# Query and gate products of a decoder's memory layer as three 16-bit products instead of one fp32 product

## The chip, the cores and the metric

The kernel runs on one core of one Trainium2 chip. The metric is the device time of one execution in microseconds (us); lower is better. Three runs of the kernel before are shown, and one execution taken with the hardware profiler.

## The reference

Two decoder layers over x of 8 batch rows x 256 tokens x 256 features, each sublayer with a layer norm of its input and a residual. In order: self-attention with 16 heads of 128; linear cross-attention over a context of 64 tokens; a feed-forward layer whose weights are rounded to 16 levels; attention over features; the memory layer; a feed-forward layer with ternary weights. The memory layer is what the change touches:

```
x = rmsnorm(hidden_states, norm_w)              # var over features, eps 1e-6, times norm_w
q = (x @ wq.T).reshape(B, L, NH, HD)            # 16 heads of 16
k = (memory_tokens @ wk.T).reshape(B, M, NH, HD)
v = (memory_tokens @ wv.T).reshape(B, M, NH, HD)
attn = jnp.einsum('blhd,bmhd->bhlm', q, k) * scale
attn = softmax(jnp.where(memory_mask[:, None, None, :], attn, -inf))
out = jnp.einsum('bhlm,bmhd->blhd', attn, v).reshape(B, L, C) @ wo.T
gate = jax.nn.sigmoid(x @ wg.T)
return gate * out
```

Here hidden_states is the layer norm of the running x, and wq and wg are 256x256.

## The kernel before

The program has two parts with a barrier between them.

**attention_part** does the self-attention: 16 heads times 4 pairs of batch rows are 64 steps (and two more, since the work of a step is spread over three). Steps 0 to 10 and 59 to 65 are written out, 11 to 58 are a loop of six rounds of eight. In step i, TensorE makes query and key products of step i, scores of step i-1 (L1124) and the value product of step i-2 (lines 75 to 77, through `pair_matmuls`), then column sums (L1153, L1155). VectorE takes the row maximum of the scores (L906), ScalarE the exponentials (L596), GpSimd splits them into exp_hi (L483) and exp_lo (L485), and VectorE adds four tiles into X (L931). TensorE's scores of the next step wait for the exponentials, whose banks they use. Much is tucked into the steps: preparing the next head's weights; the 16-level rounding (`level_part`, on VectorE, only in the loop); and, in numbered steps, scales and halves of the later layers' matrices. Such a block stands on VectorE at the end of its step, behind the four X updates. At step 60 that is L970, the lower halves of the key-value products of the linear layer. In the last steps VectorE also takes statistics of the first batch rows (L843) and normalises them (L855: tiles ctx_t, k_t). A maximum over all partitions goes through DRAM: SyncE writes the partitions' maxima out and reads them back to every partition.

A matrix "split" is scaled so that its largest value is 64, rounded to fp16 (the upper half), and the rest rounded to fp16 (the lower half). A product of two split operands is three fp16 matmuls into the same bank:

```
nc.tensor.matmul(out, lhs[0], rhs[0], start=first, stop=False)
nc.tensor.matmul(out, lhs[0], rhs[1], start=False, stop=False)
return nc.tensor.matmul(out, lhs[1], rhs[0], start=False, stop=last)
```

**streams_part** does the other five layers for each batch row alone: `lin`, `ffn`, `fat`, `mem`, `ter`. Four rows are under way at once (a group: rows 0 to 3, then 4 to 7), each with its own buffers and two of the eight banks, PA and PB. The order of the work on each engine is not written by hand. The list `work` gives the stages of one row, each with its engine, a length in us and what it comes after; `turns_by_engine` puts them in order for all rows by earliest start, and between equals by urgency, in which `LEAD * (STREAMS - b % STREAMS)` favours the earlier rows of a group.

In the memory layer a row goes so: stats, aggr, eps (VectorE), pow (GpSimd), xn (VectorE), turn (TensorE, L1688: four transposes), xt (ScalarE, L1401: two copies out of the bank, scaled by norm_w, into fp32), mem_q and mem_g (TensorE, L1673 and L1680: four fp32 matmuls of 256 columns each), qt and ge (ScalarE, L1445 and L1448). Then, for each of two tiles of 128 tokens: s (L1797, L1802: scores), max, sub, exp, sum, rd (L1623, L1626, L1452, L1630, L1633), pn (GpSimd, L1379), pt (L1810: transposes), pte, o, ote; and at the end mem_out, mem_go and mem_add. The layers `ffn` and `ter` already have a split input: ScalarE's copy to fp16 (L1405) and VectorE's lower half, `xt_stream<-banks,xt_stream` (L1527).

## Time and profile before

| | us |
|---|---|
| median of three runs | 922.98 (921.57 to 923.1) |
| the profiled execution, its own time | 921.72 |
| its span, first to last instruction | 919.9 |
| TensorE (PE) busy, matmuls | 854.1 (93%) |
| VectorE (DVE) busy | 729.0 (79%) |
| ScalarE (ACT) busy | 520.4 (57%) |
| GpSimd (POOL) busy | 369.3 (40%) |
| share of the chain that ended last: PE, DVE | 23%, 12% |

The share of busy time is an average over both parts. "Idle before" is the time in which an engine had nothing to run just ahead of an instruction, with the engine and tile that ended it. A merged row such as "1.73 PE banks L1673 x8" gives how long the chain stayed on that line: the profiler records each fp32 matmul as two, so x8 is four matmuls. Matmul rows overlap: a single one is listed with 0.27 us though the next starts 0.11 later, so lengths of products are read from the chain.

### The profile page before, as it was taken

Reading aid. Unit: us, or ns where it says so; the run is one execution under the profiler, and the core shown is the slowest. Engines: PE = TensorE matmul, PEld = TensorE weight load, DVE = VectorE, ACT = ScalarE, POOL = GpSimd, SP = SyncE. Lnnn points to the kernel's source line nnn. Section 1 sums busy time; section 2 is a strip of 40 time slices with the busy share of each in tenths; the row PEclk is TensorE's granted clock in tenths of the full one; section 3 lists DMA queues with packets and bytes.
Section 4 is the critical chain, followed back from the end, with each engine's and each line's share of the span. In section 5 each row is a group of like instructions: output and inputs, shape, how many; then the busy total and the mean of one; then the engine's idle time right before and its main releaser. Section 6 shows DMA issues by size and latency. Waiting matters only on the chain. (4 is left out here: it accounts for less than half of the span.)

```text
span 919.9 us, 18693 instructions
## 1 busy us (share of the span) xinstructions
PE 854.1 (93%) x6868; PEld 633.9 (69%) x6868; DVE 729.0 (79%) x1775; ACT 520.4 (57%) x1245; POOL 369.3 (40%) x354
## 2 busy tenths in 40 slices
PE   4788988999999999999999998999988889999786
PEld 3455766777777777777777776887855578787554
DVE  6748868878888788778887775897799779887895
ACT  1435576656665666556655745464464964535556
POOL 4103456545554455455555554053233032521410
PEclk9799999999999999999999999999999999999999
DMA  9122331011101110011000000000000010000001
GB/s 279 38 71 69 54 95 35 2 35 35 34 0 34 34 34 8 27 34 34 14 21 11 1 1 1 1 2 1 1 2 1 8 40 1 1 1 1 1 1 46
DMA packets 34722, 25.56 MB, mean 28 GB/s; under 512 B 9492, under 2 KB 31596, under 8 KB 34668
## 3 DMA queue, kind: packets, MB, share of 16 engines
q1 hardware_dynamic: 34380, 24.56, 10.2%
q8 instruction: 35, 0.57, 0.3%
q10 hardware_dynamic: 288, 0.26, 0.1%
q14 instruction: 19, 0.16, 0.1%
HBM read 22.65 MB, written 2.17 MB: 27 GB/s over the span
## 5 line engine op out<-in xcount | busy, mean ns | idle before, releaser
L483 POOL CAST exp_hi<-exp_scores 128x1024 f16<-128x1024 f32 x64 | 67.1, 1048 | 212.5 <-ACT exp_scores L596 212.5
L485 POOL TENSOR_TENSOR exp_lo<-exp_scores,exp_hi 128x1024 f16<-128x1024 f32 x64 | 140.7, 2198 | 5.1
L596 ACT ACTIVATE exp_scores<-banks,exp_bias,unscale 128x256 f32<-128x256 f32 x256 | 141.2, 560 | 2.1
L75 PE MATMUL banks<-value_out_hi,xn_t_hi 128*128 128x256 f16 x512 | 139.6, 273 | 0.2 <-DVE X L931 0.2
L77 PE MATMUL banks<-value_out_hi,xn_t_lo 128*128 128x256 f16 x512 | 139.6, 273 | 0.0
L76 PE MATMUL banks<-value_out_lo,xn_t_hi 128*128 128x256 f16 x512 | 139.6, 273 | 0.0
L1124 PE MATMUL banks<-qk 128*128 128x256 f32 x512 | 121.6, 380 | 9.0 <-ACT exp_scores L596 8.9
L1124 PEld LDWEIGHTS banks<-qk 128*128 128x128 f32 x512 | 96.6, 190 | 30.3 <-issue 9.6
L931 DVE SCALAR_TENSOR_TENSOR X<-banks,colsum,X 128x256 f32<-128x256 f32 x256 | 106.2, 477 | 11.0 <-DVE colsum L922 9.6
L575 ACT ACTIVATE qk<-banks 128x512 f32<-128x512 f32 x128 | 75.8, 601 | 57.6 <-PE banks L77 57.6
L906 DVE TENSOR_REDUCE neg_rowmax<-banks 128x4 f32<-128x1024 f32 x64 | 78.2, 1221 | 27.9 <-PE banks L1124 27.9
L75 PE MATMUL banks<-xn_t_hi,head_weights_hi 128*128 128x512 f16 x256 | 96.9, 378 | 0.6 <-issue 0.6
L77 PE MATMUL banks<-xn_t_hi,head_weights_lo 128*128 128x512 f16 x256 | 97.0, 379 | 0.0
L76 PE MATMUL banks<-xn_t_lo,head_weights_hi 128*128 128x512 f16 x256 | 96.9, 379 | 0.0
L1368 POOL TENSOR_TENSOR rstd_stream<-rstd_stream,neg_half 128x2 f32<-128x2 f32 x36 | 26.5, 737 | 138.1 <-DVE rstd_stream L1517 127.1
L592 ACT ACTIVATE exp_bias<-neg_rowmax,unscale 128x4 f32<-128x4 f32 x64 | 18.8, 293 | 100.3 <-DVE neg_rowmax L906 100.3
L76 PEld LDWEIGHTS banks<-value_out_lo,xn_t_hi 128*128 128x128 f16 x512 | 50.1, 98 | 11.8
L75 PEld LDWEIGHTS banks<-value_out_hi,xn_t_hi 128*128 128x128 f16 x512 | 50.1, 98 | 9.1 <-DVE X L931 2.5
L1379 POOL TENSOR_TENSOR big_stream<-big_stream,den_stream 128x1024 f32<-128x1024 f32 x16 | 30.4, 1903 | 60.0 <-DVE den_stream L1633 60.0
L77 PEld LDWEIGHTS banks<-value_out_hi,xn_t_lo 128*128 128x128 f16 x512 | 50.1, 98 | 5.8
L442 POOL TENSOR_TENSOR head_weights_lo<-head_weights,head_weights_hi 128x512 f16<-128x512 f32 x32 | 38.9, 1218 | 31.5 <-ACT head_weights_hi L507 31.4
L596 ACT ACTIVATION_READ_ACCUMULATOR exp_scores<-banks,exp_bias,unscale 128x1 f32 x256 | 50.7, 198 | 0.0
(251 smaller groups left out, 1964.7 us busy)
## 6 DMA issues: line engine op xcount, KB each, us to landing
head_weights<-in_wqkv_d SPq DMA_DIRECT2D x32, 128.0 KB, 3.8
weight_absmax_rows<-across_partitions SPq DMA_DIRECT2D x15, 256.0 KB, 4.3
X<-in_x_d SPq DMA_DIRECT2D x4, 512.0 KB, 7.7
head_weights<-in_wqkvt_d SPq DMA_DIRECT2D x16, 128.0 KB, 3.6
head_weights<-in_w_o_d SPq DMA_DIRECT2D x16, 128.0 KB, 3.6
out<-X SPq DMA_DIRECT2D x8, 256.0 KB, 2.1
ternary_then_kv_and_rows<-in_c_fc_d SPq DMA_DIRECT2D x1, 1024.0 KB, 5.1
ternary_then_kv_and_rows<-in_c_proj_d SPq DMA_DIRECT2D x1, 1024.0 KB, 7.9
```

The lines of the kernel that those rows point to most:

```text
L75: nc.tensor.matmul(out, lhs[0], rhs[0], start=first, stop=False)
L76: nc.tensor.matmul(out, lhs[0], rhs[1], start=False, stop=False)
L77: return nc.tensor.matmul(out, lhs[1], rhs[0], start=False, stop=last)
L442: nc.gpsimd.tensor_tensor(wlo[:, u, 2 * a:2 * a + 2], wst[:, u, 2 * a:2 * a + 2], whi[:, u, 2 * a:2 * a + 2], ALU.subtract).then_inc(wlo_r ...
L483: nc.gpsimd.tensor_copy(probh[:, s1_.par], prob[:, s1_.par]).then_inc(exph_ready, 1)
L485: nc.gpsimd.tensor_tensor(probl[:, s1_.par], prob[:, s1_.par], probh[:, s1_.par], ALU.subtract).then_inc(expl_ready, 1)
L575: nc.scalar.activation(qk[:, st.par, s, :], qk_ps[s], ACT.Copy).then_inc(qk_ready, 1)
L596: last = nc.scalar.activation(prob[:, s1_.par, t, :], sc_ps[t // ST][:, t % ST, :], ACT.Exp, bias=nbias[:, t:t + 1], scale=unscale[:, s1_. ...
L906: nc.vector.tensor_reduce(nmax[:, :], sc_both, AX.X, ALU.max, negate=True).then_inc(nmax_ready, 1)
L931: last = nc.vector.scalar_tensor_tensor(out=g.X[:, TP * s2.p + t, :], in0=xm_ps[t // ST][:, t % ST, :], scalar=csum[:, t:t + 1], in1=g.X[: ...
L1124: last = nc.tensor.matmul(sc_ps[b][:, t, :], qk[:, s1_.par, 0, q], qk[:, s1_.par, 1, kk], start=True, stop=True)
L1379: nc.gpsimd.tensor_tensor(by_head(s), by_head(s), den[s][:, t, :].unsqueeze(2).broadcast_to([P, XH, M]), ALU.mult).then_inc(mem_pn[t], 1)
```

## The change

Seven things:
- `mem_q` and `mem_g` multiply split x with split wq1 and wg1: 12 fp16 matmuls each for four fp32 ones.
- norm_w goes into the two matrices (they are multiplied by it in place), so x is copied unscaled, as in `ffn` and `ter`: ScalarE's upper half, and a new VectorE stage `mem_lo` for the lower half.
- At the end of steps 59, 61 and 62 of the head loop (`KV_HI` is 59) VectorE scales the matrices by norm_w and takes their maxima; makes scales; and makes the lower halves. ScalarE makes the upper halves in step 62. SyncE carries the maxima through DRAM.
- The scale is taken out again in the copies `mem_qt` and `mem_ge`.
- Two tables of partition maxima (`ternary_rows`, `nf4_max_rows`) now share memory with two buffers of `level_part`, which are used at other times; the new table lies there too.
- The planner's list has the new stages and lengths.
- `LEAD` goes from 2.0 to 2.5.

```
@@ -48,7 +48,7 @@
-HOP, LEAD = 0.15, 2.0
+HOP, LEAD = 0.15, 2.5
@@ -190,7 +188,14 @@
-    part = [sb("nf4_part0", [P, CHUNK * BLK], BF16), sb("nf4_part1", [P, CHUNK * BLK], BF16)]
+    part = [sb("nf4_part0_or_rows", [P, CHUNK * BLK], BF16), sb("nf4_part1_or_rows", [P, CHUNK * BLK], BF16)]
+    trows, mrows = (t[:, 0:P * 2 * 2].bitcast(F32).rearrange("p (q s) -> p q s", s=2) for t in part)
+    mem_rows = trows
+    mem_max = sb("mem_w_max", [P, 2])
+    mem_all = sb("mem_w_max_all", [P, 2])
+    mem_scale = sb("mem_w_scale", [P, 2])
+    mem_weights = [w[:, :, :].rearrange("p k n -> p (k n)") for w in (g.wq1, g.wg1)]
+    mem_parts = [[t[:, :, :].rearrange("p k n -> p (k n)") for t in pair] for pair in g.mem_halves]
@@ -434,6 +441,10 @@
+        sp.wait_ge(mem_max_ready, 2)
+        sp.dma_start(spread(6, P, 2), mem_max[:, :]).then_inc(mem_max_out, 16)
+        sp.wait_ge(mem_max_out, 16)
+        sp.dma_start(mem_rows.rearrange("p q s -> p (q s)"), gathered(6, P, 2)).then_inc(mem_max_in, 16)
@@ -605,6 +616,10 @@
+            if known(i) and i == KV_HI + 3:
+                act.wait_ge(mem_step, 5)
+                for n, (w, (hi, _)) in enumerate(zip(mem_weights, mem_parts)):
+                    nc.scalar.activation(hi, w, ACT.Copy, scale=mem_scale[:, n:n + 1]).then_inc(mem_hi_ready, 1)
@@ -964,6 +979,35 @@
+            if i == KV_HI:
+                dve.wait_ge(late_loads, 16 * len(g.small_loads))
+                for w in (g.wq1, g.wg1):
+                    for k in range(KT):
+                        nc.vector.tensor_scalar(w[:, k, :], w[:, k, :], g.normw[:, k:k + 1], None,
+                                                ALU.mult).then_inc(mem_normed, 1)
+                for n, w in enumerate(mem_weights):
+                    dve.wait_ge(mem_normed, KT * (n + 1))
+                    nc.vector.tensor_reduce(mem_max[:, n:n + 1], w, AX.X, ALU.max,
+                                            apply_absolute_value=True).then_inc(mem_max_ready, 1)
+            if i == KV_HI + 2:
+                dve.wait_ge(mem_max_in, 16)
+                nc.vector.tensor_reduce(mem_all[:, :], mem_rows.rearrange("p q s -> p s q"), AX.X,
+                                        ALU.max).then_inc(mem_step, 1)
+                dve.wait_ge(mem_step, 1)
+                nc.vector.tensor_scalar(mem_all[:, :], mem_all[:, :], 1e-30, None, ALU.max).then_inc(mem_step, 1)
+                dve.wait_ge(mem_step, 2)
+                nc.vector.reciprocal(mem_scale[:, :], mem_all[:, :]).then_inc(mem_step, 1)
+                nc.vector.tensor_scalar(g.mem_unscale[:, :], mem_all[:, :], 1.0 / SPLIT_TOP, None, ALU.mult)
+                nc.vector.tensor_scalar(g.mem_half_unscale[:, :], mem_all[:, 1:2], 0.5 / SPLIT_TOP, None,
+                                        ALU.mult).then_inc(mem_step, 1)
+                dve.wait_ge(mem_step, 3)
+                nc.vector.tensor_scalar(mem_scale[:, :], mem_scale[:, :], SPLIT_TOP, None, ALU.mult).then_inc(mem_step, 1)
+            if i == KV_HI + 3:
+                dve.wait_ge(mem_hi_ready, 2)
+                for n, (w, (hi, lo)) in enumerate(zip(mem_weights, mem_parts)):
+                    nc.vector.scalar_tensor_tensor(out=lo, in0=w, scalar=mem_scale[:, n:n + 1], in1=hi, op0=ALU.mult,
+                                                   op1=ALU.subtract)
@@ -1321,8 +1364,8 @@
-    work += norm_work("mem", "fat_add", ["xt ACT .74"])
-    work += ["mem_q PE 1.8", "mem_kbd DVE .67 fat_add", "mem_g PE 1.74 mem_xt", "mem_qt ACT .49 mem_q", "mem_ge ACT .49 mem_g"]
+    work += norm_work("mem", "fat_add", ["xt ACT .49", "lo DVE .6"])
+    work += ["mem_q PE 1.36", "mem_kbd DVE .67 fat_add", "mem_g PE 1.36 mem_lo", "mem_qt ACT .49 mem_q", "mem_ge ACT .49 mem_g"]
@@ -1396,13 +1439,8 @@
-                elif layer == "mem":
-                    for k in range(KT):
-                        last = nc.scalar.activation(xt[s][:, k, :], tiles(PA[s])[:, k, :], ACT.Copy,
-                                                    scale=g.normw[:, k:k + 1])
-                    last.then_inc(mem["xt_ready"], 1)
-                    nc.scalar.activation(xh[s], tiles(PA[s]), ACT.Copy).then_inc(ffn_hi if layer == "ffn" else ter_hi, 1)
+                    nc.scalar.activation(xh[s], tiles(PA[s]), ACT.Copy).then_inc(xt_hi[layer], 1)
@@ -1442,10 +1480,10 @@
-                nc.scalar.activation(qt[s][:, :, :], tiles(PB[s]), ACT.Copy).then_inc(mem_q, 1)
+                nc.scalar.activation(qt[s][:, :, :], tiles(PB[s]), ACT.Copy, scale=g.mem_unscale[:, 0:1]).then_inc(mem_q, 1)
-                nc.scalar.activation(gate[s][:, :, :], tiles(PA[s]), ACT.Tanh, scale=0.5).then_inc(mem_g, 1)
+                nc.scalar.activation(gate[s][:, :, :], tiles(PA[s]), ACT.Tanh, scale=g.mem_half_unscale[:, :]).then_inc(mem_g, 1)
@@ -1522,8 +1560,8 @@
-            elif part == "lo" and layer in ("ffn", "ter"):
-                dve.wait_ge(ffn_hi if layer == "ffn" else ter_hi, n[s])
+            elif part == "lo":
+                dve.wait_ge(xt_hi[layer], n[s])
@@ -1774,9 +1812,19 @@
-                features_first(PB[s], g.wq1, xt[s]).then_inc(mem_q_full, 1)
+                for m in range(KT):
+                    for k in range(KT):
+                        last = pair_matmuls(nc, tiles(PB[s])[:, m, :],
+                                            [w[:, k, m * P:(m + 1) * P] for w in g.mem_halves[0]],
+                                            [x[:, k, :] for x in (xh[s], xl[s])], k == 0, k == KT - 1)
+                last.then_inc(mem_q_full, 1)
-                tokens_first(PA[s], xt[s], g.wg1).then_inc(mem_g_full, 1)
+                for t in range(ST):
+                    for k in range(KT):
+                        last = pair_matmuls(nc, tiles(PA[s])[:, t, :],
+                                            [x[:, k, t * P:(t + 1) * P] for x in (xh[s], xl[s])],
+                                            [w[:, k, :] for w in g.mem_halves[1]], k == 0, k == KT - 1)
+                last.then_inc(mem_g_full, 1)
@@ -1980,6 +2028,9 @@
+    g.mem_halves = [[sb(f"mem_w{n}_{half}", [P, KT, D], F16) for half in ("hi", "lo")] for n in range(2)]
+    g.mem_unscale = sb("mem_w_unscale", [P, 2])
+    g.mem_half_unscale = sb("mem_w_half_unscale", [P, 1])
```

Where the new blocks stand on VectorE, in the steps 61 and 62: before, from the X updates of step 61 to the statistics of step 63 (L931 is an X update, L906 a row maximum).

```order
L931 SCALAR_TENSOR_TENSOR X<-banks,colsum,X 128x256 x4
L889 RECIPROCAL rowsum_inverse<-rowsum 128x4
L891 RECIPROCAL rowsum_inverse_halves<-rowsum 128x4
L906 TENSOR_REDUCE neg_rowmax<-banks 128x4
L919 TENSOR_SCALAR colsum_raw<-banks,unscale 128x4
L922 SCALAR_TENSOR_TENSOR colsum<-banks,unscale,colsum_raw 128x4
L931 SCALAR_TENSOR_TENSOR X<-banks,colsum,X 128x256 x4
L889 RECIPROCAL rowsum_inverse<-rowsum 128x4
L891 RECIPROCAL rowsum_inverse_halves<-rowsum 128x4
L843 BN_STATS ln_stats<-X 128x6 x4
```

And now; a maximum and a clamp of the first block stand ahead of these rows.

```order
L1000 RECIPROCAL mem_w_scale<-mem_w_max_all 128x2
L1001 TENSOR_SCALAR mem_w_unscale<-mem_w_max_all 128x2
L1002 TENSOR_SCALAR mem_w_half_unscale<-mem_w_max_all 128x1
L1005 TENSOR_SCALAR mem_w_scale<-mem_w_scale 128x2
L904 RECIPROCAL rowsum_inverse<-rowsum 128x4
L906 RECIPROCAL rowsum_inverse_halves<-rowsum 128x4
L921 TENSOR_REDUCE neg_rowmax<-banks 128x4
L934 TENSOR_SCALAR colsum_raw<-banks,unscale 128x4
L937 SCALAR_TENSOR_TENSOR colsum<-banks,unscale,colsum_raw 128x4
L946 SCALAR_TENSOR_TENSOR X<-banks,colsum,X 128x256 x4
L1009 SCALAR_TENSOR_TENSOR mem_w_lo<-wq,mem_w_scale,mem_w_hi 128x512
L1009 SCALAR_TENSOR_TENSOR mem_w_lo<-wg,mem_w_scale,mem_w_hi 128x512
```

What moved: nothing; six instructions came in behind the X updates of step 61, and two behind those of step 62, ahead of the reciprocals and of the row maximum of step 63.

On TensorE, in the memory layer of the first group, before: scores of row 1, transposes of row 3's input, scores of row 2, query and gate product of row 3, and only then row 0: its probabilities turned (L1810), scores of row 3, row 0's output (L1817).

```order
L1797 MATMUL banks<-mask_bias,ones 128x512 x2
L1802 MATMUL banks<-big_stream,qt_stream 128x256 x4
L1688 MATMUL banks<-ident,xn_stream 128x128 x4
L1797 MATMUL banks<-mask_bias,ones 128x512 x2
L1802 MATMUL banks<-big_stream,qt_stream 128x256 x4
L1673 MATMUL banks<-xt_stream,wq 128x256 x4
L1680 MATMUL banks<-wg,xt_stream 128x256 x4
L1810 MATMUL banks<-ident,big_stream 128x128 x8
L1797 MATMUL banks<-mask_bias,ones 128x512 x2
L1802 MATMUL banks<-big_stream,qt_stream 128x256 x4
L1817 MATMUL banks<-mid_stream,v 32x128 x8
```

And now, from behind row 1's scores and row 2's gate product on:

```order
L1858 MATMUL banks<-ident,big_stream 128x128 x8
L1845 MATMUL banks<-mask_bias,ones 128x512 x2
L1850 MATMUL banks<-big_stream,qt_stream 128x256 x4
L1726 MATMUL banks<-ident,xn_stream 128x128 x4
L1865 MATMUL banks<-mid_stream,v 32x128 x8
L1845 MATMUL banks<-mask_bias,ones 128x512 x2
L1850 MATMUL banks<-big_stream,qt_stream 128x256 x4
L75 MATMUL banks<-xt_stream,mem_w_hi 128x256
L76 MATMUL banks<-xt_stream,mem_w_hi 128x256
```

Row 0's probabilities (L1858) come ahead of row 2's scores, and row 0's output (L1865) and the scores of its second tile (the second L1850) ahead of row 3's query product, of which the first two matmuls are shown. The second group has the same order.

## Rows read from the trace of the kernel before

**Rows 1.** Stretches: length; busy us (instructions) of PE, PEld, DVE, ACT, POOL; clock, DMA, GB/s
```profile
50.00:540.00 490.00, 477.94 (x3855) 350.29 (x3854) 390.07 (x928) 296.13 (x814) 244.98 (x213) 1.00 0.13 31
645.00:665.00 20.00, 19.75 (x107) 16.65 (x107) 14.09 (x41) 9.10 (x20) 4.65 (x5) 1.00 0.00 1
665.00:715.00 50.00, 41.93 (x362) 28.96 (x358) 45.08 (x81) 27.69 (x37) 16.49 (x11) 1.00 0.01 1
...
840.00:890.00 50.00, 41.93 (x353) 29.60 (x353) 43.91 (x80) 26.04 (x35) 16.50 (x11) 0.97 0.00 1
```

**Rows 2.** The chain that ended last: start, us, engine and line, instructions
```profile
777.97 1.75 PE banks L1742 x16
...
836.72 1.73 PE banks L1673 x8
838.45 1.73 PE banks L1680 x8
```

**Rows 3.** Timeline of ScalarE, second group's memory layer: start us, us
```profile
821.07 0.83 ACT L1401 ACTIVATE xt_stream<-banks,normw 128x256 f32<-128x256 f32 x2
```

**Rows 4.** Groups by line, 580 to 920: busy us, mean ns; idle before
```profile
L1527 DVE TENSOR_TENSOR xt_stream<-banks,xt_stream 128x512 f16<-128x512 f32 x16 | 10.9, 680 | 0.0
...
L1405 ACT ACTIVATE xt_stream<-banks 128x512 f16<-128x512 f32 x16 | 9.5, 596 | 19.3 <-PE banks L1688 18.7
```

**Rows 5.** Timeline of the memory layer, first group: start us, us
```profile
661.27 1.90 POOL L1379 TENSOR_TENSOR big_stream<-big_stream,den_stream 128x1024 f32<-128x1024 f32 x1 [9.10 <-DVE den_stream L1633]
...
671.14 1.04 PE L1810 MATMUL banks<-ident,big_stream 128*128 128x128 f32 x8
```

**Rows 6.** Timeline of VectorE, last steps of the head loop
```profile
517.18 1.66 DVE L931 SCALAR_TENSOR_TENSOR X<-banks,colsum,X 128x256 f32<-128x256 f32 x4
...
520.95 1.22 DVE L906 TENSOR_REDUCE neg_rowmax<-banks 128x4 f32<-128x1024 f32 x1 [1.96 <-PE banks L1124]
...
537.44 1.23 DVE L906 TENSOR_REDUCE neg_rowmax<-banks 128x4 f32<-128x1024 f32 x1 [1.87 <-PE banks L1124]
...
541.01 1.66 DVE L931 SCALAR_TENSOR_TENSOR X<-banks,colsum,X 128x256 f32<-128x256 f32 x4
...
544.78 1.23 DVE L906 TENSOR_REDUCE neg_rowmax<-banks 128x4 f32<-128x1024 f32 x1
545.92 1.37 DVE L855 TENSOR_SCALAR ctx_t<-X,ln_mean_var,ln_rstd 128x256 f32<-128x256 f32 x4
...
556.16 3.22 DVE L855 TENSOR_SCALAR k_t<-X,ln_mean_var,ln_rstd 128x256 f32<-128x256 f32 x4
```

**Rows 7.** Timeline of GpSimd, the same steps
```profile
518.66 2.13 POOL L485 TENSOR_TENSOR exp_lo<-exp_scores,exp_hi 128x1024 f16<-128x1024 f32 x1
...
526.12 4.30 POOL L485 TENSOR_TENSOR exp_lo<-exp_scores,exp_hi 128x1024 f16<-128x1024 f32 x1
...
542.62 2.13 POOL L485 TENSOR_TENSOR exp_lo<-exp_scores,exp_hi 128x1024 f16<-128x1024 f32 x1
...
556.13 2.13 POOL L485 TENSOR_TENSOR exp_lo<-exp_scores,exp_hi 128x1024 f16<-128x1024 f32 x1
```

**Rows 8.** VectorE's groups by line and shape, whole span
```profile
L664 DVE TENSOR_SCALAR weight_absmax_all<-weight_absmax_all 128x4 f32<-128x4 f32 x16 | 13.0, 814 | 0.6
...
L970 DVE SCALAR_TENSOR_TENSOR ternary_then_kv_and_rows<-kv,lin_scale,ternary_then_kv_and_rows 128x128 f16<-128x128 f32 x1 | 2.6, 2630 | 0.0
...
L958 DVE TENSOR_REDUCE lin_max<-wq 128x1 f32<-128x512 f32 x1 | 0.7, 677 | 0.0
```

**Rows 9.** Timeline of TensorE's scores of steps 61 and 63, and of ScalarE's last exponential before
```profile
535.44 1.97 PE L1124 MATMUL banks<-qk 128*128 128x256 f32 x8 [0.93 <-ACT exp_scores L596]
...
548.46 0.20 ACT L596 ACTIVATION_READ_ACCUMULATOR exp_scores<-banks,exp_bias,unscale 128x1 f32 x1
...
548.81 1.97 PE L1124 MATMUL banks<-qk 128*128 128x256 f32 x8
```

**Rows 10.** DMA issues: number, size, median us to landing
```profile
weight_absmax_rows<-across_partitions SPq DMA_DIRECT2D x15, 256.0 KB, 4.3
```

9 lines of the change are left out of this document (4 added, 5 removed).

## The prediction

> **What bounds the kernel now.** I read the stretches first, to see which engine is full where. In the head loop it is TensorE: 477.94 of the 490 us from 50 to 540 [rows 1]. In the second part eight batch rows go through five layers, four at a time, and each group has two kinds of stretch. Where its memory layer begins (645 to 665), TensorE is busy 19.75 of 20 us and VectorE 14.09. Then VectorE leads: 45.08 of 50 us from 665 to 715, with TensorE at 41.93; the second group repeats this (43.91 and 41.93 from 840 to 890) [rows 1]. The chain that ended last says the same: in the first kind of stretch it is made of the products themselves, 1.73 us for the query product and 1.73 for the gate product [rows 2]. So a shorter product is worth its whole length in one stretch and nothing by itself in the other, where VectorE's length and the order decide.
>
> **The products.** Each of the 16 (a query and a gate for each batch row) is now four fp32 matmuls in 1.73 us. Sixteen matmuls of 16 bits, 256 columns wide, took 1.75 us in the feed-forward layer, 0.109 each [rows 2]. Twelve of them are 1.31 us: 0.42 saved per product, 3.4 per group, 6.7 in all.
>
> **The new lower half of x.** ScalarE's two scaled copies (0.83 us) [rows 3] become one of 0.60, as the feed-forward layer has it, and VectorE gets a subtraction of 0.68, whose input from the banks is like that of the ternary layer's [rows 4]. ScalarE wins 0.23 for each batch row, VectorE pays 0.68: 2.7 us per group. Between a row's transposes and its query product the chain grows by about 0.5 us (0.68 less 0.23, and a hand-over). TensorE has other rows' products there, so I count nothing for the wait. In the stretch where TensorE is full, VectorE had 5.9 idle us [rows 1]; two of the four subtractions fit there, the other two fall where VectorE leads: +1.4 per group.
>
> **The order.** The planner gets new lengths, and LEAD goes from 2.0 to 2.5, which favours the earlier row of a group. The second excerpt of the order shows the effect: row 0's probabilities are transposed, and its second tile's scores made, ahead of row 3's query product. In the trace those probabilities were ready when the GpSimd multiplication that starts at 661.27 and takes 1.90 us was done, but TensorE turned them only at 671.14 [rows 5]: 8 us of waiting in the queue. That work now goes in about 7 us earlier and can fill VectorE's idle time, which is 5.9 and 4.9 us in the two stretches [rows 1]. How much of these 10.8 us it fills no row shows. The bounds are 0, less if the new order stalls where the old one did not (a rival below), and about 5, half of it. I take 2.3, nearer the low end, since two more VectorE instructions now stand in front of the same softmax.
>
> Per group: six of the eight products lie in the full stretch, -2.5; the last row's two I count at nothing; +1.4; -2.3. That is -3.4, and -6.8 for both groups. Scaling the copies of query and gate by a column instead of a constant is free: both are one instruction as before.
>
> **The end of the head loop.** The splitting of the two matrices is not free. VectorE gets three blocks, each behind the four X updates of a step, and the first excerpt of the order shows two of them. GpSimd computes exp_lo at those very moments, and the trace shows what this does. Four scalings of 128x256 took 1.37 us at 545.92, but 3.22 at 556.16, when exp_lo ran from 556.13 [rows 6, 7]. The 128x128 subtraction of the key-value halves took 2.63 us, and the exp_lo beside it 4.30 where it takes 2.13 elsewhere [rows 7, 8]. So an instruction waits until the other engine's is over.
> - Step 59, from 518.8: exp_lo runs from 518.66 to 520.79 [rows 7], so the four scalings start at 520.8 and take 1.1 more; two maxima at 0.68 [rows 8] end at 523.3. The next row maximum, at 520.95 after an idle 1.96 [rows 6], comes 2.6 us later. Most of it is absorbed; some 0.8 reaches step 61, where TensorE already waited 0.93 us for the exponentials [rows 9]. Bounds 0 and 1.5; I take 0.8.
> - Step 61, from 534.7: a maximum over 256 values, well under the 0.68 of one over 512, a clamp of 0.81 like L664, and four small ones: 1.8 us. The row maximum there had been idle 1.87, after 0.56 for the exponentials [rows 6, 8]. Counted at nothing. Its input crosses SBUF through DRAM in two transfers; even two of the 4.3 us that the big one takes [rows 10] end by 532, before it is wanted. SyncE queues nothing behind them but the end.
> - Step 62, from 542.6: two lower halves of 128x512, some 0.65 each by the 0.68 of a same-sized one [rows 4], against an exp_lo that starts at 542.62 [rows 7]. Whoever is first, the second of the two ends only after exp_lo: about 546.0, 3.4 us late. Here is no slack: the row maximum at 544.78 had no idle time before it [rows 6], and the scores of the last step start at 548.81, as the exponentials end [rows 9]. Bounds: 1.4 (no contention) and 4.0. I take 3.4. ScalarE's two upper halves, 1.2 us, run while it has nothing else due.
>
> What the Trainium skill says speaks against this change: its page "SBUF — State Buffer", section "Who interferes with whom", has the port pair that VectorE and GpSimd share as an exclusive lock, taken also by a VectorE instruction with two SBUF inputs, and issue order decides who blocks. By that rule step 62 costs its 3.4, and the maxima of steps 59 and 61 are not held up; the trace agrees with the first half in the 2.63 us above, and no row here tests the second by itself.
>
> **The sum.** -6.8 + 0.8 + 3.4 = -2.6 us. The profiled execution took 921.72 (a span of 919.9 and 1.8 around it), which gives 919.1; the median of three runs is 922.98, 1.26 above the profiled one, so the forecast is **920.4 us**.
>
> **Rivals.**
> - *The order pays more* (0.22). The whole of half the idle time is filled and the lower halves of x fit in: per group -2.5 - 3.8, with the head's end -8.4: 914.6. For it: 8 us of waiting work [rows 5]. Against it: the stretch from 665 is a chain of softmax stages over few banks, not loose work.
> - *VectorE takes over* (0.30). All four subtractions per group (2.7 us) delay VectorE's softmax, TensorE's saving turns into waiting for it, and only row 0's two products (0.84), which stand before the first scores, come off. Per group +1.9, with the head's end +7.9: 930.9; the order filling part of it gives some 927. It decides from the point where VectorE's idle time between 645 and 665 is under 3 us. For it: VectorE is at 90% from 665 on [rows 1]. This is the case on the other side.
> - *The port costs less than I think* (0.06): the two lower halves slip in before exp_lo, 1.4 for 4.2 at the head's end: 917.6. Against it: the rows above.
> - *Three 16-bit matmuls are not cheaper* (0.02): with a weight load that does not overlap (0.1 each), 12 would take 2.5 us instead of 1.73, +12 us. The 16 in 1.75 us, each with its own load, speak against it.
>
> **How the numbers follow.** The forecast has 0.40; the bounds of its terms give it 917 to 924. About 0.2% is what a measurement of this kernel can tell from no change, 1.85 us here. Within the forecast's case 0.22 is faster by more than that, 0.14 within it, 0.04 slower; the order that pays and the cheap port are faster (0.28); of VectorE's case 0.05 is within and 0.25 slower; the last is slower. Together 0.50, 0.19 and 0.31. The range reaches from the order's case, 914, to most of VectorE's, 929.
>
> **What would show it.** In the new profile: query and gate products of 1.31 us in the chain; a row maximum of step 63 that starts some 5.6 us after the X updates of step 62 where it was 2.2; the head's end at about 567 instead of 563; VectorE's idle time in the memory stretch down, and each group about 3.4 us shorter. It is wrong if the head's end moves by less than 2 us, or if a group becomes longer, with TensorE waiting for VectorE's softmax.

## The result and the profile after

The changed kernel takes **923.01 us** (921.02 to 926.96, 22 runs), the kernel before 922.13 (920.07 to 923.41, 22 runs) beside it: a ratio of 1.0019, interval 1.0010 to 1.0028. It is slower by 0.9 us; the forecast was 2.6 faster. The profiled execution took 921.02, its span is 919.2; it is the fastest of the 22, so its trace shows the changed kernel at its best.

The page's busy times, where before PE had 854.1 and DVE 729.0:

```profile
PE 847.3 (92%) x6932; PEld 628.3 (68%) x6932; DVE 743.2 (81%) x1797; ACT 519.1 (56%) x1239; POOL 367.9 (40%) x354
```

TensorE has 6.8 us less to do, near 16 times 0.42, and the kernel is not faster. I divide the time at the first VectorE instruction of the second part, a product on `headmask`. For the part ahead of it I count from the row maximum of step 59: that takes out the prologue, which moves by up to 2.8 us between the traced executions (the row maximum of step 59 starts between 512.12 and 514.92). These are the two ends of that stretch, before and after.

```profile
513.49 1.23 DVE L906 TENSOR_REDUCE neg_rowmax<-banks 128x4 f32<-128x1024 f32 x1
...
564.82 1.27 DVE L1489 TENSOR_TENSOR headmask<-headmask 128x4 f32<-128x4 f32 x1 [1.65 <-PEq L1926]
```

```profile
512.25 1.23 DVE L921 TENSOR_REDUCE neg_rowmax<-banks 128x4 f32<-128x1024 f32 x1
...
568.81 1.27 DVE L1527 TENSOR_TENSOR headmask<-headmask 128x4 f32<-128x4 f32 x1 [1.69 <-PEq L1974]
```

The stretch, called the **head's end** from here on, went from 51.33 to 56.56 us: +5.2. The **second part**, from `headmask` to the start of the last update of X, went from 352.06 (564.82 to 916.88) to 347.38 (568.81 to 916.19): -4.7.

VectorE at the head's end, after; its columns are start, length, engine, line, operands, and the idle time before in brackets:

```profile
517.51 2.46 DVE L987 TENSOR_SCALAR wq<-wq,normw 128x256 f32<-128x256 f32 x2
519.89 0.60 DVE L987 TENSOR_SCALAR wg<-wg,normw 128x256 f32<-128x256 f32 x2
520.42 0.67 DVE L991 TENSOR_REDUCE mem_w_max<-wq 128x1 f32<-128x512 f32 x1
...
521.75 1.19 DVE L921 TENSOR_REDUCE neg_rowmax<-banks 128x4 f32<-128x1024 f32 x1
...
525.00 3.81 DVE L1014 SCALAR_TENSOR_TENSOR ternary_then_kv_and_rows<-kv,lin_scale,ternary_then_kv_and_rows 128x2048 f16<-128x2048 f32 x2
...
529.25 1.21 DVE L921 TENSOR_REDUCE neg_rowmax<-banks 128x4 f32<-128x1024 f32 x1
...
534.38 0.17 DVE L1000 RECIPROCAL mem_w_scale<-mem_w_max_all 128x2 f32<-128x2 f32 x1
534.46 2.09 DVE L1001 TENSOR_SCALAR mem_w_unscale<-mem_w_max_all 128x2 f32<-128x2 f32 x1
...
536.75 1.19 DVE L921 TENSOR_REDUCE neg_rowmax<-banks 128x4 f32<-128x1024 f32 x1
...
541.85 2.71 DVE L1009 SCALAR_TENSOR_TENSOR mem_w_lo<-wq,mem_w_scale,mem_w_hi 128x512 f16<-128x512 f32 x1 [0.99 <-ACT mem_w_hi L622]
544.48 0.74 DVE L1009 SCALAR_TENSOR_TENSOR mem_w_lo<-wg,mem_w_scale,mem_w_hi 128x512 f16<-128x512 f32 x1
...
547.19 1.22 DVE L921 TENSOR_REDUCE neg_rowmax<-banks 128x4 f32<-128x1024 f32 x1
...
554.72 1.23 DVE L921 TENSOR_REDUCE neg_rowmax<-banks 128x4 f32<-128x1024 f32 x1 [2.65 <-PE banks L1168]
```

GpSimd beside it:

```profile
517.41 2.14 POOL L496 TENSOR_TENSOR exp_lo<-exp_scores,exp_hi 128x1024 f16<-128x1024 f32 x1
...
534.40 2.13 POOL L496 TENSOR_TENSOR exp_lo<-exp_scores,exp_hi 128x1024 f16<-128x1024 f32 x1
541.88 2.13 POOL L496 TENSOR_TENSOR exp_lo<-exp_scores,exp_hi 128x1024 f16<-128x1024 f32 x1
```

Measured from the row maximum of step 59, the next ones came 2.0 us later than before (step 60), then 0.9 earlier (61), 0.5 later (62), 3.7 later (63) and 5.2 later (64). For before, [rows 6] has those of steps 60, 62 and 63, that of step 64 starts at 550.81, and that of step 61 is this one:

```profile
531.43 1.20 DVE L906 TENSOR_REDUCE neg_rowmax<-banks 128x4 f32<-128x1024 f32 x1
```

Three VectorE instructions end with an exp_lo or just behind it: the first pair of scalings (2.46 us, the second pair 0.60), a scaling of 128x2 at 534.46 (2.09 us, where the reciprocal before it took 0.17) and the first lower half (2.71 us, the second 0.74). The last row maximum waits 2.65 us for TensorE. Here is why, in TensorE's scores of step 62 and 63 and in stretches of 5 us (length; busy us of PE, PEld, DVE, ACT, POOL; clock):

```profile
541.03 1.89 PE L1168 MATMUL banks<-qk 128*128 128x256 f32 x8
...
551.21 3.48 PE L1168 MATMUL banks<-qk 128*128 128x256 f32 x8 [3.98 <-ACT exp_scores L607]
```

```profile
545.00:550.00 5.00, 2.05 (x33) 1.39 (x31) 4.90 (x19) 1.53 (x6) 1.21 (x2) 1.00 0.01 3
550.00:555.00 5.00, 3.79 (x11) 2.86 (x12) 2.26 (x8) 2.36 (x6) 3.32 (x3) 0.66 0.00 0
```

TensorE was busy 2.05 of 5 us and idle 3.98 before the scores; then its granted clock was 0.66 over 550 to 555, so half speed (1.2 GHz) for most of it, and the scores took 3.48 instead of 1.89 us. Before, all four stretches from 540 to 560 had clock 1.00.

The second part. The products have the length that was forecast: the query product of row 0 starts at 653.50, the gate product at 654.81, the next transposes at 656.12, 1.31 us each.

```profile
653.50 0.27 PE L75 MATMUL banks<-xt_stream,mem_w_hi 128*128 128x256 f16 x1
...
654.81 0.27 PE L75 MATMUL banks<-mem_w_hi,xt_stream 128*128 128x256 f16 x1
...
656.12 1.24 PE L1726 MATMUL banks<-ident,xn_stream 128*128 128x128 f32 x8
```

The stretches where before VectorE had 5.9 and 4.9 idle us [rows 1] (counted from `headmask` they lie 4.0 us earlier here), and VectorE's group of lower halves, whose last number is the idle time before them:

```profile
645.00:665.00 20.00, 19.75 (x142) 16.21 (x142) 17.90 (x49) 8.41 (x18) 2.09 (x3) 1.00 0.00 1
665.00:715.00 50.00, 40.80 (x378) 28.93 (x374) 46.36 (x82) 26.68 (x35) 19.01 (x13) 1.00 0.00 1
```

```profile
L1565 DVE TENSOR_TENSOR xt_stream<-banks,xt_stream 128x512 f16<-128x512 f32 x24 | 16.2, 677 | 0.7 <-ACT xt_stream L1443 0.7
```

VectorE is busy 17.90 of 20 us where it was 14.09, with 24 instead of 16 of these subtractions in the whole part, and waited only 0.7 us for their input.

### The profile page after: what moved, and what is told of

Same layout as the page of the kernel before. It is cut to its first block and busy times, and to the rows that moved or that the text cites. A ratio compares the mean times of both kernels' runs of the same rounds, so it can differ in the third digit from the quotient of the medians.

```text
span 919.2 us, 18839 instructions
## 1 busy us (share of the span) xinstructions
PE 847.3 (92%) x6932; PEld 628.3 (68%) x6932; DVE 743.2 (81%) x1797; ACT 519.1 (56%) x1239; POOL 367.9 (40%) x354
## 5 line engine op out<-in xcount | busy, mean ns | idle before, releaser
L496 POOL TENSOR_TENSOR exp_lo<-exp_scores,exp_hi 128x1024 f16<-128x1024 f32 x64 | 138.6, 2165 | 5.1
```

The costliest lines, as they stand in the source:

```text
L496: nc.gpsimd.tensor_tensor(probl[:, s1_.par], prob[:, s1_.par], probh[:, s1_.par], ALU.subtract).then_inc(expl_ready, 1)
```

## The experiments

The medians stand beside the same kernel before, measured with them: 922.13 for the change, 921.55 to 921.75 in the four batches of the others. The ratios take that out. Below, "head's end" and "second part" are read from each run's trace as above: one execution for each kernel, where a median has several.

| kernel | median, us | ratio, interval | head's end | second part |
|---|---|---|---|---|
| before | 921.6 | | 51.33 | 352.06 |
| the change | 923.01 | 1.0019 (1.0010 to 1.0028) | 56.56 | 347.38 |
| no split | 917.68 | 0.9952 (0.9935 to 0.9968) | 51.36 | 347.77 |
| split alone | 928.63 | 1.0076 (1.0062 to 1.0091) | 56.84 | 353.58 |
| change, LEAD 2.0 | 929.22 | 1.0077 (1.0062 to 1.0091) | 56.83 | 354.16 |
| before, LEAD 2.5 | 932.70 | 1.0122 (1.0107 to 1.0138) | 51.32 | 359.56 |
| blocks moved | 918.49 | 0.9955 (0.9942 to 0.9968) | 51.41 | 349.07 |
| blocks of 61, 62 moved | 917.72 | 0.9959 (0.9946 to 0.9973) | 50.83 | 348.47 |
| blocks and key-value halves moved | 916.03 | 0.9949 (0.9931 to 0.9966) | 50.24 | 347.29 |
| the same, LEAD 3.0 | 917.00 | 0.9947 (0.9929 to 0.9965) | 50.23 | 349.78 |
| 16 matmuls a product | 928.41 | 1.0069 (1.0056 to 1.0082) | 56.81 | 353.75 |
| short lower half | 922.27 | 1.0007 (0.9995 to 1.0020) | 56.71 | 346.72 |
| old order | 941.92 | 1.0222 (1.0205 to 1.0239) | 56.60 | 367.00 |
| old order, no lower half | 929.18 | 1.0068 (1.0048 to 1.0088) | 56.82 | 353.37 |
| new order alone | 922.16 | 0.9998 (0.9987 to 1.0010) | 51.31 | 352.60 |

The head's end repeats within 0.3 us between kernels that have it alike. The second part does not repeat so well: the split alone has the second part of before, stage for stage, and took 1.5 us longer, in an execution where TensorE's clock was 0.93 from 690 to 715 and from 865 to 890 (before: 1.00 and 0.98). So of the second part a difference under 1.5 us in one trace says little. The clock has a large share in this. I cut each second part into slices of 5 us and counted the time at half speed from the granted clock: 6.9 us before, 6.6 in the change, 6.9 with the new order alone, 6.8 without the split, 10.0 with the split alone, 9.9 with 16 matmuls, 10.0 in the change with LEAD 2.0, 20.5 before with LEAD 2.5, 19.7 in the old order and 13.4 there without the lower half. As an estimate, a microsecond at half speed costs at most half a microsecond (the scores above took 3.48 us for 1.89). Between executions of one kernel it shows too: of the 22 runs of the change those with a mean granted clock of 0.983 took 924.9 to 927.0 us, those with 0.987 or more 921.0 to 923.0.

### Which part costs, which earns

**No split.** The changed kernel without its three blocks, their transfers and ScalarE's upper halves; the matrices' halves hold a constant. It leaves out the scaling and splitting of the two matrices.

```
-            if i == KV_HI:
...
-            if i == KV_HI + 2:
...
-            if i == KV_HI + 3:
...
+        for t in (*mem_parts[0], *mem_parts[1], g.mem_unscale[:, :], g.mem_half_unscale[:, :]):
+            nc.gpsimd.memset(t, 0.5)
```

> The changed kernel without the three blocks and their transfers: the halves are filled with a constant at the start, so the products have the same length and wrong values; nothing else differs. Theory A (the second part earns 4.7 us, the head's end gives it back): 922.1 - 4 to 5.5, so 916.6 to 918.1. Theory B (the second part earns nothing): 922 to 923. If the blocks' cost and this gain do not add up to the change's +0.9 within 1 us, the two parts act on each other.

**Split alone.** The kernel before with the blocks, transfers and upper halves added, and nothing of it used: the second part is the old one, with its copies scaled by norm_w (which so counts twice in the output). Its diff against the kernel before is the change's own, of the parts before `streams_part`.

> The kernel before with the three blocks that scale, split and measure the two matrices at the head loop's end (and their transfers), but with the second part, its planner and its order as before; since the second part still multiplies by norm_w, that weight is applied twice. Theory A (the blocks cost what they look like in the new profile, mostly by waiting for GpSimd's exp_lo): 922.1 + 4 to 5.5, so 926 to 927.6, and in the profile the head loop ends 4 to 5 us later. Theory B (the blocks are hidden and the new profile only looks late by chance, and the second part earns nothing): 922 to 923.2.

The first came out as expected of theory A, the second 1.0 us above its range. The split costs 5.2 to 5.5 us at the head's end, and the change earns 3.9 in the second part by the medians (917.68 against 921.55), 4.3 by the traces. But the two do not add up. By the medians the split costs 7.1 us in the kernel before and 5.3 in the new one (923.01 less 917.68), and 7.1 less 3.9 is 3.2, not 0.9: by the expectation's own measure the two parts act on each other. The trace of the split alone shows where. Its row maxima in the first group keep step with those of before up to the seventh (118.85 and 118.92 us into the second part), and the eighth is 1.5 late. Between them TensorE had the same two waits in both kernels (1.76 and 0.63 us), and then its scores took this long, here and in the kernel before:

```profile
693.17 1.91 PE L1846 MATMUL banks<-big_stream,qt_stream 64*128 64x256 f32 x8
```

```profile
688.40 1.03 PE L1802 MATMUL banks<-big_stream,qt_stream 64*128 64x256 f32 x8
```

The granted clock was 0.67 from 690 to 695 in the one and 1.00 from 686 to 691 in the other; the transposes and the mask ahead of the scores lost 0.7 us as well. Why the clock fell in one execution and not in the other after the same waits, no run shows.

**LEAD back to 2.0** in the changed kernel, and **LEAD 2.5** in the kernel before, each one line:

```
-HOP, LEAD = 0.15, 2.5
+HOP, LEAD = 0.15, 2.0
```

> The changed kernel with LEAD back at 2.0. Theory A (shorter products and the planner's new lengths earn it, LEAD next to nothing): within 0.8 of the changed kernel, 922.2 to 923.8. Theory C (LEAD brings the earlier rows forward and earns at least a third of the second part's 4.7): 924.5 to 926. Theory D (LEAD costs, since the last row of each group ends later): 920 to 922.

> The kernel before with LEAD 2.5 alone. Theory A: within 0.8 of before, 921.3 to 922.9. Theory C: 919 to 920.6. Theory D: 923 to 925.

Both lose, and by more than any of the theories allowed: 6.2 us against the change, 11.1 against before. In the trace of the second, its fastest run by 4.3 us, 7.5 us are lost, and up to 6.8 of them by the estimate above are the clock's (20.5 us at half speed where before had 6.9). LEAD has no direction of its own; with the planner's lengths it picks one of many orders. Each of the two kernels has the order that suits it, and a neighbour costs more than the whole change. VectorE's lower halves show part of it, with LEAD 2.0: 5.3 us of waiting where the change has 0.7.

```profile
L1565 DVE TENSOR_TENSOR xt_stream<-banks,xt_stream 128x512 f16<-128x512 f32 x24 | 16.4, 682 | 5.3 <-ACT xt_stream L1443 5.2
```

### The head's end

**The blocks moved.** Each block stands right behind the row maximum of its own step, ahead of the X updates, instead of behind them and ahead of the row maximum of the next step (and ScalarE's upper halves ahead of the exponentials of the last step):

```
+            if known(i) and i == KV_HI:
...
+            if known(i) and i == KV_HI + 2:
...
+            if known(i) and i == KV_HI + 3:
...
             if runs(i, 2):
                 for t in range(TP):
...
-            if i == KV_HI:
...
-            if i == KV_HI + 2:
...
-            if i == KV_HI + 3:
...
```

> The changed kernel with its three VectorE blocks (steps 59, 61, 62) standing behind the next row maximum instead of ahead of it, where VectorE has idle time and no exp_lo runs on GpSimd; ScalarE's two upper halves go ahead of the exponentials of the last step. Theory A (a block costs by its place: it stands in front of a row maximum that the last scores need, and behind an exp_lo of GpSimd): the same instructions elsewhere cost 0 to 1.5 us over the kernel without them (917.7), so 917.7 to 919.2, and the second part starts 0 to 1.5 us later than the 564.7 of that kernel; the two lower halves take about 1.5 us together, none over 1.0. Rival B (blocks cost their busy length of about 7 us wherever they stand, for instance because VectorE is what the head's end waits for, or because the two upper halves on ScalarE now delay the exponentials): 921 to 923, second part at 567 or later.

What is called the next row maximum there is that of the block's own step: by the code and the trace the blocks went forward. 918.49, and a head's end of 51.41, as without the split (51.36): **the same instructions cost nothing where they stand now.** VectorE in steps 59, 61 and 62 of this kernel:

```profile
514.92 1.23 DVE L921 TENSOR_REDUCE neg_rowmax<-banks 128x4 f32<-128x1024 f32 x1
516.06 1.25 DVE L927 TENSOR_SCALAR wq<-wq,normw 128x256 f32<-128x256 f32 x2
...
534.71 0.15 DVE L941 TENSOR_SCALAR mem_w_unscale<-mem_w_max_all 128x2 f32<-128x2 f32 x1
...
538.87 1.23 DVE L921 TENSOR_REDUCE neg_rowmax<-banks 128x4 f32<-128x1024 f32 x1 [1.59 <-PE banks L1168]
540.01 0.74 DVE L949 SCALAR_TENSOR_TENSOR mem_w_lo<-wq,mem_w_scale,mem_w_hi 128x512 f16<-128x512 f32 x1
540.67 0.75 DVE L949 SCALAR_TENSOR_TENSOR mem_w_lo<-wg,mem_w_scale,mem_w_hi 128x512 f16<-128x512 f32 x1
```

The scalings take 1.25 instead of 2.46 us, the scaling of 128x2 0.15 instead of 2.09, the lower half 0.74 instead of 2.71; and from 545 to 560 TensorE's clock is 1.00 throughout. The next row maximum comes as soon as its scores are there, since a block now stands in time in which VectorE would wait for TensorE's column sums (1.89 us in step 59 and 1.78 in step 62 of the kernel before). The move changed two things at once: the blocks no longer stand directly ahead of a row maximum, and they hardly meet an exp_lo any more (the first scalings, that of 128x2 and the first lower half are together 5.1 us shorter). How much each is worth alone was not tried.

**The key-value halves moved too.** The two subtractions of step 60, in the kernel before as well, go behind the row maximum of step 60 likewise.

```
+            if known(i) and i == KV_HI + 1:
+                dve.wait_ge(kv_halves, 2)
...
             if runs(i, 2):
...
-            if i == KV_HI + 1:
-                dve.wait_ge(kv_halves, 2)
...
```

> As the kernel before it, and the two lower halves of the key-value products (in both kernels, old and new, at the end of step 60: 4.9 and 3.8 us beside an exp_lo) moved behind the row maximum of step 61 too. Theory A: these two instructions pay the same price in the old kernel as the new blocks, so 1 to 2.5 us more come off: 915.5 to 918 and a second part that starts at 562.5 to 564.5. Rival B (TensorE's work of the last steps, not VectorE's, sets the end once nothing stands ahead of the maxima): no difference from the kernel before it, within 0.7 us.

916.03, a head's end of 50.24, 1.1 us shorter than that of the kernel before. They take 3.02 us (4.89 with the blocks alone moved, 3.81 in the change), and the row maximum of step 61 comes 15.45 us after that of step 59, at 512.25 here; before that took 17.94 (531.43 less 513.49):

```profile
520.85 3.02 DVE L954 SCALAR_TENSOR_TENSOR ternary_then_kv_and_rows<-kv,lin_scale,ternary_then_kv_and_rows 128x2048 f16<-128x2048 f32 x2
...
527.70 1.22 DVE L921 TENSOR_REDUCE neg_rowmax<-banks 128x4 f32<-128x1024 f32 x1
```

This kernel beats both: 0.9949 of the time before (0.9931 to 0.9966).

**Only the blocks of steps 61 and 62 moved**, as above; that of step 59 in its place.

> The changed kernel with the blocks of steps 61 and 62 moved behind the row maximum, and that of step 59 (scalings and maxima, 2.46 us for the first two scalings beside an exp_lo) left in its place. Theory A1 (step 59 costs nothing, since the row maximum after it had idle time before it; all of the head end's 5.2 us are those of step 62 and the half clock behind it): the stretch from the row maximum of step 59 to the second part's first instruction is 51.3 to 51.8 us (56.6 in the changed kernel, 51.4 with all three moved), the time 918 to 919.3. Rival A2 (step 59 carries the 0.8 of the prediction or more into step 61): 52.2 or longer, 919.3 to 920.5.

917.72, a head's end of 50.83: not longer than with all three moved, but 0.6 shorter. The block of step 59 is late by itself (the row maximum of step 60 starts at 521.68, 2.0 later than before by the same count), and then pays it back. The two key-value subtractions of step 60 now start 0.78 us ahead of GpSimd's exp_hi (525.70), which takes 2.47 instead of 1.04 us, and exp_lo starts only at 528.25; before, they met exp_lo. They take 3.81 instead of 4.89 us.

```profile
524.92 3.81 DVE L1014 SCALAR_TENSOR_TENSOR ternary_then_kv_and_rows<-kv,lin_scale,ternary_then_kv_and_rows 128x2048 f16<-128x2048 f32 x2
```

### The second part

**Sixteen matmuls.** The changed kernel with a fourth product, lower half by lower half:

```
-                                            [x[:, k, :] for x in (xh[s], xl[s])], k == 0, k == KT - 1)
+                                            [x[:, k, :] for x in (xh[s], xl[s])], k == 0, False)
+                        last = nc.tensor.matmul(tiles(PB[s])[:, m, :], g.mem_halves[0][1][:, k, m * P:(m + 1) * P],
+                                                xl[s][:, k, :], start=False, stop=k == KT - 1)
...
```

> The changed kernel with a fourth fp16 product (lower half by lower half) in each query and gate product, so that each is 16 matmuls and 1.75 us, as long as the fp32 ones were; order and planner as in the change. Theory A (the products are the path where TensorE is full: six of eight per group, 0.44 us each): +2.6 us per group, +5.3 in all, 928.3 (927 to 929.5). Rival C (the gain of the second part is the order's, and the lengths are off the path, which the kernel with LEAD 2.0 suggests): 0 to +1.5, 923 to 924.5.

928.41: +5.4. A product is 1.75 us long here (655.00 to 656.75), 0.44 more, 7.0 in all. In the new order most of that counts: 5.4 us by the medians, 4.6 by the ratios, 6.4 by the traces, of which the clock can be 1.7.

**A short lower half**: 8 of its 512 columns, and the matmuls read the upper half for it.

```
-                nc.vector.tensor_tensor(xl[s], tiles(PA[s]), xh[s], ALU.subtract).then_inc(ln["xt_ready"], 1)
+                some = (lambda x: x[:, :, 0:4]) if layer == "mem" else (lambda x: x)
+                nc.vector.tensor_tensor(some(xl[s]), some(tiles(PA[s])), some(xh[s]),
+                                        ALU.subtract).then_inc(ln["xt_ready"], 1)
...
-                                            [x[:, k, :] for x in (xh[s], xl[s])], k == 0, k == KT - 1)
+                                            [x[:, k, :] for x in (xh[s], xh[s])], k == 0, k == KT - 1)
```

> The changed kernel with the memory layer's lower half of x cut to 8 of 512 columns (about 0.1 instead of 0.68 us on VectorE), the matmuls reading the upper half in its place; everything else, semaphores and order too, as in the change. Leaves out the lower half of x. Theory A (two of four per group lie where VectorE leads): -1.4 us per group less what is left, about -2.4 in all: 920.6 (919.5 to 921.5). Rival D (VectorE bounds the group and all four count): -2.3 per group, 918.4 (917.5 to 919). Rival C (the path goes elsewhere): 922.5 to 923.3.

922.27, 0.7 less than the change (0.66 by the traces, 1.1 by the ratios), where 2.4 less was expected. The intervals of the two ratios overlap, so this can't be told from nothing. The eight subtractions together cost about 0.7 us if anything, not the 2.8 that I gave them.

**The new order alone.** The kernel before, its order on every engine that of the change (the planner's list and LEAD of the change, its lower halves then taken out):

```
+    turns["DVE"] = [x for x in turns["DVE"] if x[1] != "mem_lo"]
```

> The kernel before with the changed kernel's order on every engine (new list, LEAD 2.5), and nothing else of the change: fp32 products, copies scaled by norm_w, no split, no lower half of x. The forecast's own term (the order earns 2.3 us per group): 917 to 918.5, a second part of 347.5. Theory E (the order earns nothing by itself; it only has room for the lower half): -1 to +2 us, 920.5 to 924, a second part of 351 to 354. Rival F (an order planned for short products loses with long ones, as LEAD 2.5 alone did): 926 or more.

922.16 against 921.66, ratio 0.9998 (0.9987 to 1.0010). **The new order by itself is worth nothing.** Its own trace shows the trade. VectorE's first and last row maximum of the first group in it, and then in the kernel before:

```profile
652.56 1.22 DVE L1624 TENSOR_REDUCE den_stream<-banks 128x16 f32<-128x1024 f32 x1 [1.74 <-PE banks L1803]
...
691.10 1.22 DVE L1624 TENSOR_REDUCE den_stream<-banks 128x16 f32<-128x1024 f32 x1
```

```profile
655.92 1.23 DVE L1623 TENSOR_REDUCE den_stream<-banks 128x16 f32<-128x1024 f32 x1 [1.78 <-PE banks L1802]
...
689.48 1.23 DVE L1623 TENSOR_REDUCE den_stream<-banks 128x16 f32<-128x1024 f32 x1 [0.64 <-PE banks L1802]
```

Against the start of each second part (563.45 and 564.82) the first comes at 89.1 instead of 91.1, 2.0 us earlier, and the last at 127.7 instead of 124.7, 3.0 later: the first row wins, and the last one pays.

**The old order under the new work.** The planner's old list and LEAD; the lower half put in by hand where its input could be ready.

```
-HOP, LEAD = 0.15, 2.5
+HOP, LEAD = 0.15, 2.0
...
+    for b in range(B):
+        stage_before = ((b + 3, "fat_eps"), (b + 1, "mem_aggr"), (b + 1, "fat_p"), (b, "mem_kbd"))[b % STREAMS]
+        turns["DVE"].insert(turns["DVE"].index(stage_before) + 1, (b, "mem_lo"))
```

> The changed kernel with the second part in the old order on every engine (the list and LEAD of before), only the lower half of x put in where its input is ready. Theory C (the shorter products earn their length only in the new order, as the kernel with LEAD 2.0 suggests): 927.5 to 930, a second part of 353 to 355 us. Rival D (the order is worth little by itself and the products earn their 0.42 each in the old one too; the kernel with LEAD 2.0 lost because its order was a third one): 922.5 to 925, a second part of 347 to 350 us.

941.92, far outside both. The group of lower halves has 13.4 us of waiting, and TensorE then waits for VectorE:

```profile
L1568 DVE TENSOR_TENSOR xt_stream<-banks,xt_stream 128x512 f16<-128x512 f32 x24 | 16.4, 684 | 13.4 <-ACT xt_stream L1446 13.4
```

```profile
664.27 0.74 PE L1809 MATMUL banks<-ident,big_stream 128*128 128x128 f32 x4 [3.80 <-DVE big_stream L1633]
```

Part of this is my placing: another one would have waited less. So I took the lower half out, and with it everything that VectorE does more. It leaves out the lower half of x.

```
-    for b in range(B):
-        stage_before = ((b + 3, "fat_eps"), (b + 1, "mem_aggr"), (b + 1, "fat_p"), (b, "mem_kbd"))[b % STREAMS]
-        turns["DVE"].insert(turns["DVE"].index(stage_before) + 1, (b, "mem_lo"))
...
-                pe.wait_ge(mem["xt_ready"], n[s])
+                pe.wait_ge(xt_hi["mem"], n[s])
...
-                                            [x[:, k, :] for x in (xh[s], xl[s])], k == 0, k == KT - 1)
+                                            [x[:, k, :] for x in (xh[s], xh[s])], k == 0, k == KT - 1)
```

> The kernel with the old order (941.9), without the memory layer's lower half of x: its VectorE stage is left out and the products read the upper half in its place, so nothing of VectorE or ScalarE is longer or later than in the kernel before. Theory E (the old order has no gap for the lower half: VectorE stood idle 13.4 us in front of it, with everything behind it in the queue; without it the shorter products earn in the old order what was forecast, 5 to 6.7 us): a second part of 345.5 to 347.5 us, and with the head end's 5.2 a time of 920.5 to 923. Rival C (the shorter products earn nothing in the old order, since VectorE or the order sets the pace there): a second part of 350.5 to 353, 925.5 to 928.5.

929.18, second part 353.37: my theory E falls, and rival C comes nearest (both numbers lie a little above its ranges). The split alone, with the old order and the long products, takes 928.63 and has 353.58. **In the old order the kernel is not faster for shorter products.** The traces show where the time goes. TensorE in this kernel (the transposes of probabilities are L1858) and then in the kernel before (L1810), at the same place of the program:

```profile
674.65 1.04 PE L1858 MATMUL banks<-ident,big_stream 128*128 128x128 f32 x8
...
678.78 0.65 PE L1865 MATMUL banks<-mid_stream,v 128*32 128x128 f32 x16 [1.84 <-ACT mid_stream L1494]
679.36 1.93 PE L1858 MATMUL banks<-ident,big_stream 128*128 128x128 f32 x8
681.22 0.61 PE L1845 MATMUL banks<-mask_bias,ones 64*128 64x512 bf16 x2
681.62 1.64 PE L1850 MATMUL banks<-big_stream,qt_stream 64*128 64x256 f32 x8
```

```profile
673.95 0.64 PE L1817 MATMUL banks<-mid_stream,v 128*32 128x128 f32 x16 [0.58 <-ACT mid_stream L1456]
674.52 1.09 PE L1810 MATMUL banks<-ident,big_stream 128*128 128x128 f32 x8
```

And VectorE's next row maximum in each:

```profile
683.32 1.23 DVE L1661 TENSOR_REDUCE den_stream<-banks 128x16 f32<-128x1024 f32 x1 [1.85 <-PE banks L1850]
```

```profile
676.85 1.23 DVE L1623 TENSOR_REDUCE den_stream<-banks 128x16 f32<-128x1024 f32 x1 [0.23 <-PE banks L1802]
```

TensorE was 1.84 us idle instead of 0.58, since its work was done sooner while ScalarE's was not; then it ran at half clock for a while (the granted clock is 0.94 from 675 to 680 and 0.71 from 680 to 685; 1.93 us for 1.09, 0.61 for 0.39, 1.64 for 1.03: 1.7 us more), and VectorE waited 1.85 us for the scores instead of 0.23. By the row maxima, each against the start of its second part, this kernel was 0.9 us ahead before that place (678.99 less 570.56, before 674.15 less 564.82) and 0.7 behind after it (683.32, before 676.85). That the half clock did this was read from the rows, not tried by itself. By the count above this second part has 3.4 us more at half speed than that of the split alone, at most 1.7 us: without them the products might have earned that much of their 6.7 in the old order too.

**LEAD 3.0** with the blocks and key-value halves moved:

> The kernel with all blocks and the key-value halves moved (916.03), with LEAD 3.0 for 2.5. The planner then puts 46 of TensorE's 284 stages and 128 of VectorE's 544 in another place. Theory C (the second part's length hangs on details of the order, and LEAD has no direction): anything from 914 to 925, most likely slower than 916. Rival (a larger LEAD goes on paying, as from 2.0 to 2.5 with these lengths): 910 to 914.

917.00 with a range that overlaps that of 916.03 (914.21 to 919.87 and 914.62 to 920.62): no difference shown, and no gain from a larger LEAD.

## Why the prediction was wrong

The direction was wrong by 3.5 us: forecast -2.6, measured +0.9. Term by term:

- **The order, -4.6: this is the step that failed.** It measured 0 (0.9998; the interval, 0.9987 to 1.0010, is 1.2 us to the faster side). I read 8 us of waiting work and 10.8 us of idle VectorE [rows 1, 5] and took part of it as fillable. But alone the order only trades: it brings the first group's first softmax 2.0 us forward and its last 3.0 back. It is worth something only with the short products: the two together earn 3.9 us (no split against before) to 5.6 (the change against the split alone), either of them alone none that was measured. Pricing them apart, from one profile, was the mistake.
- **The products, -5.0**: 0.42 each was exact. Made 7.0 us longer again, they cost 5.4, near the six of eight that I counted. Right, but only in this order.
- **The lower half of x, +2.8**: 0.7, not clear of nothing. The planner had set it into idle time that I gave to the order: VectorE's busy time from 645 to 665 rose by 3.8 us, and in the trace no query or gate product of the memory layer waited for it. With the new order alone VectorE is busy 16.43 us in such a stretch (644 to 664), so 2.3 of the 3.8 are the order's.
- **The copies of query and gate, 0**: not free. On ScalarE each takes 0.69 us, scaled by a column, where it took 0.60; 1.4 us for all 16, most of what the shorter copy of x saves. No run shows whether that reached the end.
- **Step 59, +0.8**: about -0.9. The scalings waited for exp_lo just as said (2.46 us), the row maximum came 2.0 us late, and the slack I named took it; beyond that the key-value subtractions moved out of their own wait.
- **Step 61, 0**: +1.5. The block was expected to take 1.8 us and took 3.2 (533.43 to 536.68), since a scaling of two columns met the exp_lo at 534.40 and took 2.09. I had used the overlap rule for the big instructions and not for the small ones.
- **Step 62, +3.4**: +3.1. The mechanism was right, with one more link: the first lower half waited 0.99 us for ScalarE's upper half.
- **Not in the sum**: TensorE stood idle for 3.98 us behind step 62, its granted clock was 0.66 from 550 to 555, and the last row maximum came another 1.5 us later.

Head's end: -0.9 + 1.5 + 3.1 + 1.5 = +5.2, forecast +4.2. That it came so near is partly luck: step 59 was 1.7 too high, step 61 and the clock together 3.0 too low. Second part: -4.7, forecast -6.8. The sum is +0.5, measured +0.9. The rival on the other side (VectorE takes over) was not it either, though its sign came: VectorE's idle time from 645 to 665 is 2.1 us, under the 3 that I had named. That bound was wrong, since VectorE had room for the subtractions and the second part became shorter. The Trainium skill's page "SBUF — State Buffer", section "Who interferes with whom", counts a scaling of one SBUF operand among the VectorE instructions that can take the port pair shared with GpSimd; the trace agrees with 2.46 and 2.09 us beside exp_lo and 1.25 and 0.15 without. Its statement that a reduction on this chip never contends had one small test, and the trace agrees: the maximum over the gathered table (533.43, 0.41 us) ran beside GpSimd's exp_hi (533.28, 1.04 us) and took 0.40 with GpSimd idle, in the kernel with the blocks moved, while the clamp right behind it took 0.47 instead of 0.17.

## What to carry to other kernels

Work tucked into a pipelined loop costs by its place, not by its length: 5.2 us ahead of the reduction on which the next step hangs and beside GpSimd's instructions, nothing right behind the reduction of the step itself, where it hardly met them; which of the two did it was not separated. Look for such a place for what is already there, too (1.1 us here). And where an order is planned, do not add up what a shorter stage and a new order would each save: time both together, since a shorter stage in the old order can end as idle time and a lower clock, here with none of 6.7 us left.

## What the hardware showed that I had not expected

- A scaling of 128x2 in fp32 took 2.09 us beside a GpSimd instruction that had started 0.06 us before it; the same one took 0.15 elsewhere. So even this smallest of scalings waited for the whole of the other engine's instruction.
- The lower half that was issued at 541.85, 0.03 us ahead of the exp_lo at 541.88, ended behind it (544.56 against 544.01), and exp_lo kept its 2.13 us. At the key-value halves of step 60 it was the other way round in the kernel before: the first started at 526.09, exp_lo at 526.12, and exp_lo took 4.30 us [rows 7, 8].
- In the slice from 550 to 555 us TensorE's granted clock was below 0.9 in every trace with the blocks in the change's place (seven kernels: 0.50 to 0.70), and 1.00 from 545 to 560 in the eight without. A wait that makes TensorE idle was paid twice there, the second time by the scores that took 3.48 us for 1.89.
